# Delta-rule sandwich layer on one core: filter tiles between leading chunks, a second bank pair in the first stage, and a new order of every queue

## The reference, cut to what matters

```python
x = x + layernorm(attn(layernorm(x)))
x = x + layernorm(ffn(layernorm(x)))

# attn: 4 heads of 64; v, q, k by projection, 4-tap convolution and silu
q, k, v = (silu(conv4(h @ W.T)) for W in (Wq, Wk, Wv)); beta = sigmoid(h @ Wb.T)
delta = delta_rule(l2norm(q), l2norm(k), v, beta)        # state (64 x 64) per head, in order of time
local_s, local_m, local_l = fir(v, 3 taps), fir(v, 15 taps), fir(v, 63 taps)
probs = softmax((h @ gate_w + gate_b) / exp(log_temp)); probs = probs * (1 - 5 eps) + eps
o = probs . (local_s, local_m, local_l, delta, v);  attn = rmsnorm(o) @ Wo.T
# ffn: r = sigmoid(mix(mu_r) @ Wr.T), out = r * (relu(mix(mu_k) @ Wk.T)^2 @ Wv.T)
```

## Time and profile before

| | us |
|---|---|
| median of 3 runs | 615.87 |
| lowest and highest | 606.55, 617.87 |
| profiled execution | 611.72, of which the span from first to last instruction is 609.9 |
| busy in the span | PE 512.3, DVE 465.3, POOL 336.4, ACT 276.6 |
| TensorE's mean granted clock | 0.943 of full speed |

### The profile page before, as it was taken

One profiled execution on the slowest core, in us unless ns is written; L12 is line 12 of the kernel. 1 busy time (PEld: TensorE's weight loads), 2 busy tenths in 40 slices (PEclk: granted clock), 3 DMA queues, 4 the chain that ended last, 5 costly groups with the idle time before them and its releaser, 6 DMA issues.

```text
span 609.9 us, 23551 instructions
## 1 busy us (share of the span) xinstructions
PE 512.3 (84%) x9580; PEld 407.8 (67%) x9580; DVE 465.3 (76%) x1182; ACT 276.6 (45%) x688; POOL 336.4 (55%) x408
## 2 busy tenths in 40 slices
PE   2888848999889789798999979899787899888764
PEld 1666636666667567677777767777666777777553
DVE  3788684655589673788899989899768879889863
ACT  5788882111355443435455444454342444433421
POOL 9966202877702440486626378464278776566622
PEclk9999997999999795899999999999888899999978
DMA  9729444699344425341444624165343244333101
GB/s 286 204 71 258 144 139 121 156 225 227 64 73 75 81 63 100 52 72 37 98 88 92 121 52 80 44 120 105 67 72 69 51 104 76 70 80 80 37 17 35
DMA packets 155707, 61.10 MB, mean 100 GB/s; under 512 B 125009, under 2 KB 147409, under 8 KB 155601
## 3 DMA queue, kind: packets, MB, share of 16 engines
q1 hardware_dynamic: 155600, 59.61, 44.5%
HBM read 40.62 MB, written 18.95 MB: 98 GB/s over the span
## 4 chain that ended last, share of the span: by engine, by line
PE 29%; DVE 23%; issue 17%; POOL 13%; SPq 7%; DMA 6%; ACT 3%; POOLq 0%; DVEq 0%; ACTq 0%
PE bank L1864 6%; PE bank L1639 5%; DVE cva L1126 4%; DVE arena L1236 3%; PE bank L1553 3%; POOL arena L659 3%; PE bank L1901 3%; DVE arena L1350 3%; PE bank L1718 2%; DVE arena L1365 2%; DVE arena L1338 2%; POOL seq L650 2%; POOL seq L561 2%; PE bank L1758 2%; POOL seq L648 2%
## 5 line engine op out<-in xcount | busy, mean ns | idle before, releaser
L659 POOL TENSOR_TENSOR arena<-arena,neg_half 128x2 f32<-128x2 f32 (+1 forms) x64 | 61.2, 956 | 148.4 <-DVE arena L1325 88.1
L1236 DVE SCALAR_TENSOR_TENSOR arena<-bank,small,arena 128x256 f32<-128x256 f32 x192 | 89.9, 481 | 15.5 <-ACT arena L898 10.6
L1210 DVE TENSOR_TENSOR seq<-bank,seq 128x384 f32<-128x384 f32 x64 | 35.2, 556 | 30.3 <-PE bank L1639 19.4
L606 POOL TENSOR_TENSOR arena<-seq,powers 128x16 f32<-128x16 f32 x16 | 48.6, 3040 | 17.0 <-DVE seq L1252 17.0
L1639 PE MATMUL bank<-arena 128*64 128x192 f32 x512 | 50.4, 340 | 3.9 <-DVE seq L1210 1.6
L1126 DVE SCALAR_TENSOR_TENSOR cva<-bank,small,cva 128x256 f32<-128x256 f32 x96 | 40.3, 477 | 15.1 <-ACT cva L775 14.8
L577 POOL TENSOR_TENSOR seq<-seq 128x256 f32<-128x256 f32 x32 | 23.3, 729 | 48.2 <-DVE seq L1210 48.2
L1639 PEld LDWEIGHTS bank<-arena 128*64 128x64 f32 x512 | 35.4, 140 | 13.4 <-issue 6.3
L1350 DVE TENSOR_SCALAR arena<-arena 128x256 f32<-128x256 f32 x64 | 31.7, 536 | 16.0 <-POOL arena L659 16.0
L898 ACT ACTIVATE arena<-bank,small 128x256 f32<-128x256 f32 x64 | 29.7, 467 | 26.2 <-PE bank L1718 26.2
L1718 PE MATMUL bank<-arena,w_k 128*128 128x268 f32 x128 | 34.5, 412 | 4.4 <-issue 3.1
(11 more groups left out here) (170 smaller groups left out, 1364.5 us busy)
## 6 DMA issues: line engine op xcount, KB each, us to landing
arena<-v_scratch SPq DMA_DIRECT2D x64, 128.0 KB, 3.3
arena<-fl SPq DMA_DIRECT2D x32, 192.0 KB, 6.4
arena<-fms SPq DMA_DIRECT2D x32, 192.0 KB, 6.8
arena<-xnT_scratch SPq DMA_DIRECT2D x32, 134.0 KB, 3.1
arena<-x SPq DMA_DIRECT2D x32, 128.0 KB, 2.9
gram_scratch<-arena SPq DMA_DIRECT2D x32, 128.0 KB, 2.4
out<-arena SPq DMA_DIRECT2D x32, 128.0 KB
xnT_scratch<-seq SPq DMA_DIRECT2D x2, 1027.0 KB, 6.7
```

The source lines that it names most:

```text
L606: pool.tensor_tensor(rk, ssel[:, slot_of(n)], powers[:, :, :], ALU.pow).then_inc(s["norms"], 1)
L659: pool.tensor_tensor(dst, src, half8 if k == U else neg_half[:, 0:k], ALU.pow).then_inc(s[dst_sem], 1)
L1210: nc.vector.tensor_tensor(fprod[:, q % (2 * FPAIRS), :], bank[fir_bank(q)][:, 0:2 * ROW], fgate[:, q // (TILES // 2), :], ALU.mult).then_i ...
L1236: nc.vector.scalar_tensor_tensor(cv[:, t], ps[:, :, j:j + C], conv_w[:, 1 - t // 2, t % 2, j:j + 1], cv[:, t], ALU.mult, ALU.add).then_inc ...
```

## The change

What it does, part by part:

- First stage: `a_proj` of odd quarters writes banks 7 and 1 (`a_bank`), and their taps go to a second row buffer `cvx` (`a_row`). `a_proj` waits for the convolution two quarters back. `a_xT` uses bank 0 alone. The first four normalised tiles are made by DVE (`a_first`). The bias and 1/temperature of the gates are applied by ACT as it copies the gate logits (`a_gT_out`, now with function Identity, bias and scale), so the 10 instructions of L1174 go; the constants are laid out per gate for it, and three small DVE instructions stand after the first convolution (`gates_prepared`). `gates_mixed` holds the second part of the softmax, after the last convolution.
- ACT's `fgate` copies stand ahead of its wait for the stores, and DVE's wait for the stores goes.
- Leading chunks: `sumsq` writes bank 5, in which chunk m's q1 is projected, so it waits for the convolution of q1, and the next `proj(m, 1, 1)` waits for `ssel`. `sumsq(m)` stands between `gram(m, 0)` and `gram(m, 1)`.
- The second half of the filter tiles: on PE, 8 pairs of tiles stand before `gram(0, 0)`, and then two pairs between each `gram` and the next, up to chunk 3.
- All queues have a new order, the loop and the tail too.

```diff
+        def a_bank(q, oh):
+            return bank[(2, 3, 7, 1)[2 * (q % 2) + oh]]
+        def a_row(q, oh):
+            return (cvx if q % 2 else cva)[:, oh, :]
         def sum_bank(m):
-            return bank[6 if m < FREE else 1]
+            return bank[5 if m < FREE else 1]
@@ SP, lead_step
-                if n + 4 < 0 and solving(n + 4) is not None:
-                    solved_store(solving(n + 4))
+                if n + 2 < 0 and solving(n + 2) is not None:
+                    solved_store(solving(n + 2))
+                if 0 <= n + 10 < 8:
+                    block_in(n + 10)
@@ ACT
             def a_gT_out(b):
-                act.activation(gT, bank[6][:, 0:2 * P], ACT.Copy).then_inc(s["a_gT"], 1)
+                act.wait_ge(s["g_step"], G_READY)
+                act.activation(gT, bank[6][:, 0:2 * P], ACT.Identity, bias=gate_bias, scale=inv_temp).then_inc(s["a_gT"], 1)
@@ DVE
+            def a_first(b):
+                if b == 0:
+                    dve.wait_ge(s["a_rs"], 1)
+                    for m in range(4):
+                        nc.vector.tensor_scalar(xna[:, m, :], xa2[0][:, m, :], mv_a[:, m, 0:1], rs_a[:, m:m + 1],
+                                                ALU.subtract, ALU.mult).then_inc(s["a_first"], 1)
-                for g in range(5):
-                    for pr in range(PAIRS):
-                        last = nc.vector.tensor_scalar(gates[:, g, pr, :], gates[:, g, pr, :], gb[:, pr, g:g + 1],
-                                                       inv_temp[:, pr:pr + 1], ALU.add, ALU.mult)
-            for par in ("even", "odd"):
-                dve.wait_ge(s[f"xT_{par}_stored"], 16 * 2)
-                dve.wait_ge(s[f"vb_{par}_stored"], 64 * 2)
@@ PE
             def a_proj(b, q):
-                    if b or q:
-                        pe.wait_ge(s["a_conv"], b * 24 + 6 * (q - 1) + 5 + oh)
+                    if 4 * b + q >= 2:
+                        pe.wait_ge(s["a_conv"], b * 24 + 6 * (q - 2) + 5 + oh)
             def lead_step(n):
-                if FIRST <= n + 151 < FIRST + 8:
-                    fir_tiles(n + 151, 0)
-                if 0 <= n + 28 < 8:
-                    gram(n + 28, 0)
+                if 0 <= n + 20 < 8:
+                    proj(n + 20, 1, 0)
+                    proj(n + 20, 1, 1)
+                if FIRST <= n + 9 < FIRST + 8:
+                    fir_tiles(n + 9, 1)
+                if 0 <= n + 21 < 8:
+                    proj(n + 21, 0, 1)
+                    proj(n + 21, 0, 0)
+                if 0 <= n + 20 < 8:
+                    gram(n + 20, 0)
+                    sumsq(n + 20, 1)
+                    gram(n + 20, 1)
+                if FIRST <= n + 10 < FIRST + 8:
+                    fir_tiles(n + 10, 0)
```

More of the change, by code:

```diff
@@ L536, in _ @@
+            for n in range(-225, 23):
                 lead_step(n)
@@ L748, in _ @@
-            for n in range(-170, 22):
+                if n + 107 < 0:
+                    solve_part(n + 107, 0)
+                if 0 <= n + 85 < 1:
+                    direct(n + 85)
+                if 0 <= n + 60 < 1:
+                    norms(n + 60)
+                if FIRST <= n + 211 < FIRST + 8:
+                    fir_sums(n + 211, 0)
+                    fir_sums(n + 211, 1)
+                if n + 151 == -1:
+                    scan_zero(n + 151)
+                if n + 84 < 0:
+                    solve_part(n + 84, 1)
+                    solve_part(n + 84, 2)
@@ L874, in _ @@
                 act.wait_ge(s[f"vb_{par}_stored"], 64 * 2)
[L875 to L880 removed]
+            act.wait_ge(s["fgate_mm"], PAIRS + 1)
             for pr in range(PAIRS):
@@ L1025, in chunk_step @@
-            def chunk_step(n):
+                if 0 <= n + 4 < 1:
+                    low_out(n + 4)
+                if 0 <= n + 11 < 8:
+                    gram_out(n + 11, 1)
+                if 0 <= n < 1:
+                    values(n)
+                if 0 <= n + 12 < 8:
+                    tap(n + 12, 2)
+                    silu(n + 12, 0)
+                    tap(n + 12, 3)
+                    silu(n + 12, 2)
+                if 0 <= n + 2 < 1:
+                    ktok_out(n + 2)
@@ L1091, in tail_step @@
                     xf_out(n - 2)
-            for n in range(-170, 22):
+                if 9 <= n < N:
+                    off_out(n)
+                if 8 <= n - 1 < N:
+                    oT_out(n - 1)
+                if 9 <= n < N:
+                    values(n)
+                    ktok_out(n)
+            for n in range(-225, 23):
                 lead_step(n)
@@ L1969, in chunk_step @@
                 if 8 <= n + 8 < N:
-                    gram(n + 8, 1)
+                    sumsq(n + 8, 1)
+                if 1 <= n + 1 < 9:
+                    off_second(n + 1)
                 if 8 <= n + 9 < N:
```

865 lines of the change are left out of this document (413 added, 452 removed).

## The result

The changed kernel takes 604.9 us (median of 20 runs, 602.0 to 608.0) where the kernel before takes 614.9 us in the same session (20 runs, 606.6 to 621.0). The ratio is 0.9865 with a 95% interval of 0.9844 to 0.9886: 1.35% faster. The ratio leaves out slow runs, those over 1.5% above the fastest of their kernel, while the medians count all, and by them the difference is 10.1 us. Either way it is about half of what I forecast, 17.6 us in the sum and 595 us as a time. The profiled execution has a span of 601.0 us against 609.9.

What follows compares the result with a forecast made beforehand. It took hand-overs between nearly full engines as the bound. Terms -1.5, -5.7, -1.4, -6.0, -2.0, +1.0, -2.0 sum to -17.6 us, from 611.7 to 594.1, stated as 595; 588 to 602 at 0.50, wider range 584 to 611.

Steps and rivals of the forecast that it cites:

- Part 1: Start of the kernel: PE's first transposes wait less for normalised tiles, as DVE makes them instead of POOL; -1.5 us.
- Part 2: First stage: two bank pairs loosen the quarters' hand-overs and the gates lose instructions, 2.75 us of it; together -5.7 us.
- Part 3: From last convolution to filters: ACT's fgate copy no longer waits for the stores' DMA, low clock assumed; -1.4 us.
- Part 4: Filters and leading chunks: two pairs move behind `gram(3, 1)`, -3.6, and a third of the gaps closes, 2.4; -6.0 us.
- Part 5: First solve: solution stored ahead of the next block, -2.0 us; values and norms now behind the solve, +1.0 us.
- ACT's tables: Rival, first stage: Identity among silus makes ACT reload tables, 10.3 us for two loads a batch, time 605; chance 0.02.
- Part 6: Loop and tail in new order: a fifth of the loop's idle time goes, -2.0 us over 8 steps; tail 0.
- a new wait in the loop: Rival: PE waits each loop step for DVE's late subtraction (`off_in`); at 2.5 us a step 614; 610 and up, chance 0.11.
- little of it arrives: Rival: only the gates, start, fgate wait (5.6 us) and moved tile work (3.6) are gained; 602 to 610, chance 0.22.

Runs made afterwards that it cites:

- e6: Changed kernel with the first stage's projections back in one pair of banks and the taps in one row buffer: 611.0 us.
- e1: Changed kernel with the loop and the tail in the order of the kernel before, on all five engines: 596.8 us.
- e5: Changed kernel with all filter tiles, products and block copies ahead of the first leading chunk again on PE, DVE and ACT: 620.2 us.
- e4: Changed kernel with, in POOL's tail steps, the output norm's power and the row norms ahead of the solve's first part: 608.2 us.
- e3: Changed kernel with only SP's order of issuing the loop's and the tail's DMAs put back to that of before: 603.8 us.
- e13: Changed kernel with the tail of before on all engines and the loop of before on PE and DVE together: 616.6 us.
- e7: Changed kernel with only the loop in the order of before, on all five engines, the tail staying new: 606.5 us.
- e12: On top of e1, ACT's last two silus of the first stage put ahead of the gates' tanh and exponential: 597.8 us.
- e14: Changed kernel with the tail of before on all engines and, in the new loop, DVE's read-out of the sums of squares ahead of the residual: 604.6 us.

## Why the prediction was right and where it failed

**Part 1** was right in mechanism: the first convolution starts at 14.09 instead of 16.34, 2.2 us earlier (forecast 1.5).

**Part 2** had the batch at 17.4 us; batches 1 and 2 take 17.4 (steps of 4.3, 3.4, 4.3, 5.4 for the forecast 4.4, 3.4, 4.0, 5.6). Batch 0 takes 19.3 us (quarters at 14.09, 20.29, 23.65, 27.98, the next batch at 33.36), where before it took 18.8, so the 0.7 us forecast for it did not come. The last convolution starts 6.4 us earlier, where parts 1 and 2 promised 7.2. What I did not see is shown by e6: under the new order of ACT the second pair, with its second row, is worth 7.5 us, not the 3 left over without the gates. With one pair the last convolution comes later than before although the gates' 2.75 us are gone, so the new order needs the second pair.

**Part 3** gained its fgate wait (L888 waits for PE alone now; no idle time is ended by a DMA as in the earlier trace rows), and the clock stayed at the low level as chosen: 0.50 at 89 to 93 us. The gate products took 2.78 us, as in the earlier trace rows. But the seam, "silu, the last two `a_win` and ACT's copies take 4.0 us and they stay", was 1.5 us short: the exponential's end and the load for silu (1.28 us) came to stand between convolution and silu, and it is 5.5 us. The third pair of tiles, due near 94, starts near 96.4.

**Part 4** was under-sized. From the third pair to the end of `gram(3, 1)` the change took off 8.6 us (6.3 by the third pair, 14.9 at the gram), not 6.0; a mixed step is 10.6 us (grams at 145.9, 156.6, 167.2, 177.8), inside the forecast's 10.3 to 11. I had closed a third of 8 us of gaps; less the 3.6 us of work moved behind the gram, 5.0 us of them closed, five eighths. The two errors cancel, and that is luck: the sum had `gram(3, 1)` done at 179.2, and it was done at 178.9.

**Part 5**: the solve starts 15.3 us earlier (190.01), as the sum up to there says, and the solution is stored at 205.70, ahead of the next block's load. PE's first instruction of `low_first(0)` is at 215.03, 36.1 us behind `gram(3, 1)`, where 37 were due and 39.4 had been: 18.1 us of gain, so these parts gave 3 us more than promised by then. From there to residual(0) are 30.6 us (before 30.8), at a granted clock of 0.88 from 217 to 246 us, where before it was 0.72. This stretch already belongs to the loop's order and not to part 5 alone. With the same lead and the old loop, e1 took 33.8 us, 3.0 more than the kernel before; that would be the forecast's bound for the values and norms that now stand behind the solve (0 to +3.3, taken as 1.0), but no run moves them alone.

**ACT's tables**: the rival had Identity among silus bring loads. The profile after has four loads in all, as before, none of them at the Identity's line. As the Trainium skill (ScalarE: Activation LUTs, Table sets: the hidden batching unit) has it, such functions lie in every set; the trace agrees, with 0 loads for it.

**Part 6 is the step that failed.** It said -2.0 us for the loop and 0 for the tail, and the trace shows +9.4 us behind residual(0), +9.3 behind `low_first(0)`. An undisturbed loop step even gained: 23.5 us, 23.85 before. That this looks like the forecast's 23.3 is partly an accident, for the 23.5 us that the prediction calls a steady step is the length of the window in the earlier trace rows; the steps measured at the residual were 23.8 to 23.9. Tail steps are 18.2 instead of 17.9. The error was to compare the queues in a steady step and multiply by eight. The loss sits in the steps that aren't steady: the step behind a block's arrival (3 to 4, 27.8 for 25.9), the one where the loop has just begun (1 to 2, 25.3 for 23.9), and the step from loop to tail (32.1 for 27.1), for which I had no term at all. The rival "a new wait in the loop" named the cost's kind and order of size, with 1.5 to 2.5 us a step and `off_in` as the place; the waits that came are others (the projection for the sums' read-out, the block's DMA, the power behind the solve), and they strike a few steps of sixteen. For the attribution e1 stands: with loop and tail as before the time is 596.8, 8 us below the changed kernel and 18.7 below the kernel before in its session, where parts 1 to 5 had promised 15.6. That this is within 2 us of the forecast of 595 is partly luck, since the forecast was counted from the profiled 611.7 and the medians of the kernel before lie 2 to 5 us above that.

The measured 604.9 falls where the rival "little of it arrives" had its range, 602 to 610, but for another reason than that rival's: the first stage and the mixing did arrive, 14.9 us at `gram(3, 1)`, and e5 and e6 each lose 6 us or more without their part.

The clock adds to the loss. The read-out's wait of 4.10 us on PE was followed by 4 us at 0.60, and the next two halves took 1.4 us more than in the earlier trace rows. The Trainium skill (TensorE: Matmul & The Clock Gate, HAM oscillation) describes that waits between bursts of matmuls bring the low clock back; the loop's 0.96 against e1's 1.00 agrees.

## What to carry to other kernels

An order written out by hand over five in-order queues is one object. Cost it at its steady step, but then walk it once through every step that differs: the first, the last, the one with the rare work in it, the seam between two stages; that is where the new order met things that are late. And when one engine's part of a new order looks guilty, putting that one back can be worse than either whole order (616.6 against 601.8 and 596.8); take back the stage on all engines at once. A wait that an edit only moves to another place or engine (6.82 us for 3.19, 14.0 for 9.5) did not shorten the kernel by going. And before one instruction's start is used as a mark in two kernels, see that the same calls stand ahead of it in both.

## What the runs showed of the hardware

Within one kernel a lower granted clock mostly goes with a longer time, but not by a fixed rate. e4's four runs go from 0.924 and a span of 611.0 us to 0.946 and 604.1, e3's from 0.935 and 605.0 to 0.950 and 598.1, some 3 to 5 us for each 0.01. The changed kernel's 20 runs give 1.7 us for each 0.01 as a fitted line, and two of them were granted 0.937 and 0.946 with spans of 601.0 and 604.1, the other way round.

The stretch ahead of residual(0) differs between kernels, and there it follows the order, not chance. From the second part of `low_first(0)` to residual(0), in the changed kernel, e1 and e13 (windows view of each; the clock is the last number but two):

```profile
217.37:245.62 28.25, 22.67 (x742) 18.97 (x744) 15.85 (x37) 11.54 (x34) 9.08 (x9) 0.88 0.40 71
220.26:251.73 31.47, 27.51 (x704) 22.49 (x708) 17.40 (x41) 11.70 (x36) 11.17 (x12) 0.65 0.37 64
217.27:249.69 32.42, 25.04 (x763) 20.47 (x764) 18.49 (x41) 12.65 (x38) 12.42 (x18) 0.89 0.41 72
```

All three traces with the whole loop old (e1, e7, e12) were granted 0.65 here and took 31.5 to 31.6 us; ten others with DVE's loop new (all but e14, where `low_first(0)` runs in one part) were granted 0.77 to 0.94 and took 27.6 to 29.7. The low clock does not explain the length alone: e13, with the old loop on PE and DVE only, was granted 0.89 and took 32.4 us. With DVE's old order residual(0) has four more calls ahead of it.
